# Layer norms with means in four PSUM banks and fewer filler matmuls, and the first shifted inputs of a local attention sent by the stage before it

## What is computed

```python
x = x + retention(layernorm(x))              # 16 heads, causal, no softmax
x = x + cross(layernorm(x), context)         # 16 heads, sigmoid scores
z = layernorm(x)
for l in range(2):
    h = shift_token(z)                       # upper half of the features moved one token on
    z = z + local_attention(h @ wqkv) @ wo   # windows of 64, 8 heads of 64, softmax
    h = layernorm(shift_token(z)) * lg + lb
    a, g = split(h @ w1 + b1)
    z = z + (a * gelu(g)) @ w2 + b2
x = x + z
```

## Time and profile before

| | |
|---|---|
| median of 3 runs | 1876.77 us (1872.91 to 1878.39) |
| profiled execution, its own time | 1873.96 us |
| its span | 1872.1 us |
| mean granted TensorE clock | 0.976 of 2.4 GHz |
| busy: TensorE, ScalarE, VectorE, GpSimd | 92%, 78%, 55%, 24% |

### The profile page before, as it was taken

One profiled execution on the slowest core, in us unless ns is written; L12 is line 12 of the kernel. 1 busy time (PEld: TensorE's weight loads), 2 busy tenths in 40 slices (PEclk: granted clock), 3 DMA queues, 4 the chain that ended last, 5 costly groups with the idle time before them and its releaser, 6 DMA issues. The chain is left out here.

```text
span 1872.1 us, 67917 instructions
## 1 busy us (share of the span) xinstructions
PE 1713.8 (92%) x28036; PEld 1024.3 (55%) x28036; DVE 1025.8 (55%) x3242; ACT 1462.7 (78%) x2635; POOL 445.5 (24%) x353
## 2 busy tenths in 40 slices
PE   7898799999998999999999968999989789889888
PEld 4675455555554555555555435666653256656633
DVE  4444633333332334333331069999964499899844
ACT  3332699999997999999999848999972389989832
POOL 1003100000000000000000047777710377767300
PEclk9998999999998999999999989999999999999999
DMA  1000211111111111111110021111110011111100
GB/s 59 3 3 26 104 48 50 60 43 61 62 62 35 57 54 49 56 62 62 52 39 17 27 82 27 35 31 25 28 27 0 11 27 24 35 29 26 32 15 34
DMA packets 47469, 73.88 MB, mean 39 GB/s; under 512 B 8400, under 2 KB 38224, under 8 KB 47184
## 3 DMA queue, kind: packets, MB, share of 16 engines
q1 hardware_dynamic: 47184, 69.85, 12.1%
HBM read 21.08 MB, written 2.10 MB: 12 GB/s over the span
## 5 line engine op out<-in xcount | busy, mean ns | idle before, releaser
L638 ACT ACTIVATE x_probs<-x_pss 128x1024 f32<-128x1024 f32 x832 | 806.3, 1021 | 51.7 <-PE x_pss L559 36.7
L573 PE MATMUL x_acc<-x_probs,x_v 128*32 128x256 f32 x6656 | 437.7, 380 | 0.1
L559 PE MATMUL x_pss<-x_qx,x_kx 32*128 32x256 bf16 x9984 | 348.4, 270 | 14.3 <-issue 6.5
L559 PEld LDWEIGHTS x_pss<-x_qx,x_kx 32*128 32x128 bf16 x9984 | 221.4, 93 | 200.0 <-ACT x_probs L638 179.8
L573 PEld LDWEIGHTS x_acc<-x_probs,x_v 128*32 128x32 f32 x6656 | 206.6, 110 | 93.3 <-issue 9.1
L1244 ACT ACTIVATE l_prob<-l_sim,l_neg_top,l_inv_norm 128x128 f32<-128x128 f32 x512 | 245.7, 487 | 5.7 <-DVE l_neg_top L1138 4.6
L685 DVE COPY x_vnext<-x_psp 128x128 f32<-128x128 f32 (+1 forms) x199 | 59.2, 298 | 315.3 <-PE x_psp L537 312.2
L870 POOL TENSOR_TENSOR l_turned_half<-l_raw,l_tabB 128x512 f32<-128x512 f32 x128 | 181.5, 1439 | 69.9 <-ACT l_raw L1203 69.6
L614 POOL COPY x_zq<-zT 128x256 f32 (+1 forms) x15 | 6.0, 400 | 763.7 <-PE x_psp L544 695.4
L880 POOL TENSOR_TENSOR l_direct<-l_direct,l_turned_half 128x1024 f32<-128x1024 f32 x64 | 156.1, 2439 | 0.0
L1130 DVE CUSTOM_DVE_ANT_0 l_sim<-l_pss,w_window 128x128 f32<-128x128 f32 x512 | 118.0, 285 | 4.3 <-issue 2.9
(11 more groups left out here) (177 smaller groups left out, 2636.6 us busy)
## 6 DMA issues: line engine op xcount, KB each, us to landing
x_kx<-x_kp SPq DMA_DIRECT2D x96, 208.0 KB, 2.3
x_cT<-in_context SPq DMA_DIRECT2D x16, 832.0 KB, 4.5
x_qx<-x_qp SPq DMA_DIRECT2D x48, 192.0 KB, 3.0
l_vmid<-l_vt SPq DMA_DIRECT2D x64, 128.0 KB, 2.3
xT<-in_x SPq DMA_DIRECT2D x8, 256.0 KB, 4.9
shifted<-zT SPq DMA_DIRECT2D x32, 64.0 KB, 2.0
hs<-zT SPq DMA_DIRECT2D x32, 64.0 KB, 2.0
out_x<-xT SPq DMA_DIRECT2D x8, 256.0 KB, 2.0
```

Of the source, the lines that this page charges most:

```text
L559: ins = pe.matmul(pss[bank(k, 2 * p + r // 2)][:, r % 2, e, :], kx[par][rows, g, j * P:(j + 1) * P], qx[par][rows, g, a * S:(a + 1) * S], ...
L573: ins = pe.matmul(acc[32 * r:32 * r + 32, 0:S], v[:, j, g, r, :], probs[SLOT[p]][r // 2][:, r % 2, e, :], start=(u == 0), stop=(u == UNITS ...
L638: act.activation(probs[SLOT[p]][y][:, :, :, :], pss[bank(k, 2 * p + y)][:, :, :, :], ACT.Sigmoid, scale=HD ** -0.5).then_inc(weighed, 1)
```

## The change

Means of norm 1 and norm 3 and of both gate stages go to four banks, the two of `mean` and the first two of `wide`; norm 2, which uses all of `wide` for its projection, keeps two. In all three norms the 8 filler matmuls ahead of `widen(0)` are gone. In the gate stages the wait for the second refinement moves behind `widen(0, 0)`. The copies for batches 0 to 3 of a local attention are issued by SyncE in the stage before: in norm 3 behind the weight loads and before the wait for them, in gate 0 as chunks 0 and 1 are added. The `landed` semaphores become four that both layers share.

```diff
+def shift_in(sp, shifted, zT, landed, n):
+    sp.dma_start(shifted[n % 4][0:64, :], zT[0:64, n * S:(n + 1) * S]).then_inc(landed[n % 4], 16)
+    sp.dma_start(shifted[n % 4][64:P, 1:S], zT[64:P, n * S:(n + 1) * S - 1]).then_inc(landed[n % 4], 16)
...
 # layer_norm
+        means = mean if project is not None else [*mean, wide[0], wide[1]]
+        MB = len(means)
...
                 for tile, dram in loads:
                     sp.dma_start(tile, dram).then_inc(landed, 16)
+                if next_shift is not None:
+                    shifted, batches_landed = next_shift
+                    sp.wait_ge(cleared, len(zeros))
+                    for n in range(4):
+                        sp.wait_ge(normed, base + n // 2 + 1)
+                        shift_in(sp, shifted, dst, batches_landed, n)
                 if loads:
                     sp.wait_ge(landed, 16 * len(loads))
...
-                if n >= 2:
-                    pe.wait_ge(centered, base + n - 1)
-                pe.matmul(mean[n % 2][:, :], ones_mean[:, :], src[:, at[n]], start=True, stop=True).then_inc(mean_ready, 1)
+                if n >= MB:
+                    pe.wait_ge(centered, base + n - MB + 1)
+                pe.matmul(means[n % MB][:, :], ones_mean[:, :], src[:, at[n]], start=True, stop=True).then_inc(mean_ready, 1)
...
             variances(1)
-            keep_warm(WARM)
             widen(0)
             keep_warm(WARM)
             widen(1)
...
 # local_attention
             def shift(n):
-                if n >= 4:
-                    sp.wait_ge(v_projected, 2 * n - 6)
...
+                sp.wait_ge(v_projected, 2 * n - 6)
+                shift_in(sp, hs, zT, landed, n)
...
-            for n in range(4):
-                shift(n)
             for n in range(B):
                 middle(n)
...
-                        pe.wait_ge(landed[r], 32 * (q + 1))
+                        pe.wait_ge(landed[r], 32 * (q + 1) + 32 * (B // 4) * layer)
...
 # norm_and_gate
+        means = [*mean, wide[0], wide[1]]
...
+        if next_shift is not None:
+            @block.sync
+            def _(sp):
+                for n in range(4):
+                    sp.wait_ge(added, runs + n // 2 + 1)
+                    shift_in(sp, next_shift[0], zT, next_shift[1], n)
...
-                if n >= 2:
-                    pe.wait_ge(centered, base + n - 1)
-                pe.matmul(mean[n % 2][:, :], ones_mean[:, :], hs[:, at[n]], start=True, stop=True).then_inc(mean_ready, 1)
+                if n >= 4:
+                    pe.wait_ge(centered, base + n - 3)
+                pe.matmul(means[n % 4][:, :], ones_mean[:, :], hs[:, at[n]], start=True, stop=True).then_inc(mean_ready, 1)
...
                     widen(0, 0)
+                    pe.wait_ge(newton, (run * NG + 1) * 2 + 2)
                     for c in range(4):
                         spread_out(1, c)
                     widen(0, 1)
...
-            pe.wait_ge(newton, (run * NG + 1) * 2 + 2)
             pe.wait_ge(centered, base + NCH)
             chunks(pe, chunk)
```

More of the change, by code:

```diff
@@ L36 @@
 NEG = -3.0e38
+def shift_in(sp, shifted, zT, landed, n):
+    sp.dma_start(shifted[n % 4][0:64, :], zT[0:64, n * S:(n + 1) * S]).then_inc(landed[n % 4], 16)
+    sp.dma_start(shifted[n % 4][64:P, 1:S], zT[64:P, n * S:(n + 1) * S - 1]).then_inc(landed[n % 4], 16)
 def layer_norm(nc, tag, norms, src, dst, loads=(), zeros=(), gain=None, source=None,
-               project=None, arrived=None):
+               project=None, arrived=None, next_shift=None):
     ones_mean, eps, pick, run = norms["ones_mean"], norms["eps"], norms["pick"], norms["runs"]
@@ L171, in _ @@
                 dve.wait_ge(mean_ready, base + n + 1)
-                dve.tensor_tensor(dst[:, at[n]], src[:, at[n]], mean[n % 2][:, :], ALU.subtract).then_inc(centered, 1)
+                dve.tensor_tensor(dst[:, at[n]], src[:, at[n]], means[n % MB][:, :], ALU.subtract).then_inc(centered, 1)
             refine(0)
@@ L740, in _, with local_attention @@
                 add(B - 1, c)
-def local_attention(nc, tag, zT, w, hs, moved_to, moved):
+def local_attention(nc, tag, zT, w, hs, moved_to, moved, landed, layer):
     KEYS = [[(0, P, 0, P)], [(WINDOW, WINDOW + P, 0, WINDOW), (P, S, WINDOW, P)]]
@@ L781, in local_attention @@
         pso = ps("pso", [P, PH, P])
-        ready, landed = sem("ready"), [sem(f"landed{r}") for r in range(4)]
+        ready = sem("ready")
         q_projected, k_projected, squared = sem("q_projected"), sem("k_projected"), sem("squared")
@@ L827, in shift @@
             def shift(n):
-                if n >= 4:
-                    sp.wait_ge(v_projected, 2 * n - 6)
-                sp.dma_start(hs[n % 4][0:64, :], zT[0:64, n * S:(n + 1) * S]).then_inc(landed[n % 4], 16)
-                sp.dma_start(hs[n % 4][64:P, 1:S], zT[64:P, n * S:(n + 1) * S - 1]).then_inc(landed[n % 4], 16)
+                sp.wait_ge(v_projected, 2 * n - 6)
+                shift_in(sp, hs, zT, landed, n)
             def middle(n):
@@ L1278, in _, with norm_and_gate @@
             turns(act, turn)
-def norm_and_gate(nc, tag, norms, gates, zT, hs, w, moved, layer, xT=None, out=None, stored=None):
+def norm_and_gate(nc, tag, norms, gates, zT, hs, w, moved, layer, xT=None, out=None, stored=None, next_shift=None):
     ones_mean, eps, pick, run = norms["ones_mean"], norms["eps"], norms["pick"], norms["runs"]
@@ L1441, in _ @@
                 dve.wait_ge(mean_ready, base + n + 1)
-                dve.tensor_tensor(hs[:, at[n]], hs[:, at[n]], mean[n % 2][:, :], ALU.subtract).then_inc(centered, 1)
+                dve.tensor_tensor(hs[:, at[n]], hs[:, at[n]], means[n % 4][:, :], ALU.subtract).then_inc(centered, 1)
             refine(0)
@@ L1496, in build @@
         stored = ctx.enter_context(nc.semaphore("stored"))
+        batches_landed = [ctx.enter_context(nc.semaphore(f"batch_landed{r}")) for r in range(4)]
         gates = [ctx.enter_context(nc.semaphore(f"gate_{n}")) for n in (
@@ L1546, in build @@
             layer_norm(nc, "n3", norms, xT, zT, loads,
-                       [x[:, :] for x in shifted])
+                       [x[:, :] for x in shifted], next_shift=(shifted, batches_landed))
             for l, w in enumerate(ws):
-                local_attention(nc, f"l{l}", zT, w, shifted, hs, moved)
+                local_attention(nc, f"l{l}", zT, w, shifted, hs, moved, batches_landed, l)
                 if l + 1 < DEPTH:
-                    norm_and_gate(nc, f"g{l}", norms, gates, zT, hs, w, moved, l)
+                    norm_and_gate(nc, f"g{l}", norms, gates, zT, hs, w, moved, l, next_shift=(shifted, batches_landed))
                 else:
```

## The result

The changed kernel took 1858.44 us (median of 5 runs, 1854.96 to 1863.45) against 1876.77: ratio 0.9893 with the 95% interval 0.9869 to 0.9916. The profiled execution took 1858.44 us, with a span of 1856.6 (before 1872.1) and a mean granted clock of 0.978.

What follows compares the result with a forecast made beforehand. Bound by short waits in the norms, gates and local attention starts, any gain there shifting what follows. Terms 2.2 + 1.96 + 2.3 + 2.4 + 2.5 + 0.65 = 12.0 us, from median 1876.77 to 1864.8; range 1859 to 1871.5.

Steps and rivals of the forecast that it cites:

- Norms, the filler: All three norms: the filler alone holds back group 0's spread; removing it gains 1.96 us in each.
- Norm 3 and its SyncE: Norm 3 into local attention 0: SyncE's copies end the stage, but the first matmul starts sooner; gain 2.3 us.
- the term of 2.5: Start of local attention 1: copies issued in gate 0 remove TensorE's 2.57 us wait for data; gain 2.5 us.
- if the shorter idle time spares this, 0.85 more: Start of local attention 1: 0.85 us extra if shorter idle time avoids the clock's fall near TensorE's restart.
- the term of 2.4: Gate 0: 0.3 us by order, 0.5 by banks and 1.65 by a spared low clock; taken as 2.4 us.
- The 0.3 for the order: Gates: running chunk 0's matmuls ahead of the wait for the second refinement wins at most 0.3 us.
- The 1.65 for the spared low clock: Gate 0: chunk 0's matmuls no longer run into the low clock after TensorE's idle time; 1.65 us.
- Gate 1: 0.65 forecast: Gate of layer 1: at most 0.3 us by order together with 0.4 by the banks, taken as 0.65 us.
- Norm 2: 1.96, which cross attention inherits as a shift: Norm 2 ends 1.96 us sooner without its filler, and cross attention merely starts that much earlier.
- The first: Rival: full queue in norm 3, low clock in gate 0, half of layer 1's start lost; 7.2 us gain, chance 0.20.
- The second: Rival: attention's pipeline absorbs the starts, SyncE eats norm 3; about 4.5 us gain, 1872.3, chance 0.10.
- The third: Rival: clock falls inside each norm without filler, 4.6 us in each, near 20 in all; 1884.8, chance 0.04.

Runs made afterwards that it cites:

- e1: Kernel before, with only the 8 filler matmuls ahead of the first spread removed in the three norms: 1872.27 us, ratio 0.9974.
- e6: The changed kernel measured once more, nothing altered: 1859.52 us, ratio 0.9907 to the kernel before.
- e8: Changed kernel, but norm 3 issues only batch 0's two copies and local attention 0 the other six at its start: 1857.5 us, ratio 0.9904.
- e11: e8 with `widen(0, 1)` put ahead of group 1's spread in the gates: 1853.54 us, ratio 0.9886.
- e2: Kernel before, with only the means in four banks (norms 1 and 3, both gates): 1871.69 us, ratio 0.9976.
- e5: The kernel before measured once more, nothing altered: 1879.14 us, ratio 1.0004.
- e3: Kernel before, with only the shift copies issued in the stage before: 1867.58 us, ratio 0.9944.
- e4: Kernel before, with only the gates' wait for the second refinement moved behind the first chunk's matmuls: 1876.14 us, ratio 0.998.
- e9: Kernel before, with the first 8 fillers of each norm made one column wide, same instruction count: 1881.35 us, ratio 1.0038.
- e10: Kernel before, with 8 one-column matmuls added behind each norm's second spread: 1878.36 us, ratio 1.0019.
- e7: Changed kernel, with 8 one-column matmuls added behind each norm's second spread: 1859.99 us, ratio 0.9928.
- e12: e11 with the norms' second 8 fillers dropped too: 1858.35 us, ratio 0.9902.

## Why the prediction was right and where it failed

**Norms, the filler: right.** From the start of the second variances to the end of norm 2 it is 10.79 us before and 8.81 after: 1.98 for the forecast 1.96. By whole stages, norm 2 measured 26.90 to 27.90 us without the first fillers (after, e1, e6, e8, e11), 28.85 to 29.82 with them (before, e2 to e5): means 27.6 and 29.4, a gain of 1.8, with the scatter of what stands ahead of the variances. Norm 1, with the banks, went from a mean of 29.11 (before, e3, e4, e5) to 26.43 (after, e6, e8, e11): 2.7 for 2.2, the surplus falling to the banks, where 0.4 to 0.7 was seen for 0.3.

**Norm 3 and its SyncE: the mechanism right, the size a little low.** From the start of norm 3 to the first matmul of local attention it was 20.97 + 2.62 = 23.59 us before and 20.63 + 0.04 = 20.67 after: 2.9 for 2.3. The 0.6 more is SyncE's weight loads, whose last issue ended 14.9 us into the stage, where it had been 15.5 (1087.19 - 1071.65). Over the 14 profiles it ended 13.7 to 16.2 us into the stage, so this part is chance. No run shows the full queue that the prediction names as a bound: no issue of a copy sent ahead took longer than 0.61 us. Norm 3 and local attention 0 together went from a mean of 320.2 (before, e5) to 317.0 (after, e6), 3.2.

**Local attention 1: the term of 2.5 was too small.** In seven kernels without the copies ahead, POOL's first product comes 5.83 to 7.17 us into the stage (mean 6.60); in seven with them 2.80 or 2.81. That is 3.8. I had most of the rest and put it aside: "if the shorter idle time spares this, 0.85 more". It spares it in all seven, and in four of the six others the start took longer than in the profile that I had. How much of it reaches the end of the stage is less sure: the means of the whole stage are 308.4 and 305.2 us, 3.2 less, and the kernels that ran it with 17.1 us at the low clock differ by 2.4 (before and e9 against e3, e6 and e8).

**Gate 0: the term of 2.4 was too large.** The gates with 3.4 us at the low clock, and none of it at chunk 0 except in the kernel before, took 84.92 to 85.12 without the change (before, e1, e3, e10) and 84.63 to 84.71 with it (after, e7, e8, e11, e12): 0.3, which is the banks. The 0.3 for the order is zero by e4 against e3. The 1.65 for the spared low clock was booked as certain. Its size was right (1.66 in e4), but before the edit the clock fell there in 5 of 14 gates only, so it is worth about 0.6 us a gate on average, in both layers (estimate: 1.65 times 5/14). The changed kernel has its low clock at the first means instead, which is chance too, and so the two profiles differ by only 0.45. The Trainium skill, page "TensorE: Matmul & The Clock Gate", section "Why this matters for your kernels", asks for no long idle gaps between bursts of matmuls. The traces agree as far as they go: behind 2.57 us the clock fell at chunk 0 in 5 gates of 14, behind 0.92 us in none of 14.

**Gate 1: 0.65 forecast,** 0.25 by the banks; the rest of the 1.84 between the two profiles goes with 3.6 us less at the low clock.

**"Norm 2: 1.96, which cross attention inherits as a shift": this is the step that failed.** The sum put the untouched stages at nothing, and cross attention is not shifted rigidly. In the kernels with the old split (8 or 9 records, then a second pause of 1.9 to 2.9 us: before, e2, e3, e4, e5, e7, e9) the batch behind the loop's return takes 59.97 to 62.11 us, mean 61.10; in those without it (after, e1, e6, e8, e10, e11, e12; a second pause of 0.40 to 0.98 in three, none over 0.2 in four) 56.82 to 59.41, mean 57.99. The gain of 3.1 had no term in my sum. Part of it is clock: the first group has 8.3 us low on average and the second 4.9. At the same 6.8 us low it is 60.4 (e2, e5, e7, e9) against 59.1 (after, e1, e8), 1.3 us. The other 1.8 goes with the clock; that the longer pause brings it about is likely, but no run separates the two. e7, e9 and e10 show that the number of TensorE instructions in front of the loop decides: with the old number the split is there though the fillers do other work; with eight fewer or eight more in each norm it is gone. The instruction blocks on q8 show the wait itself: in all ten kernels with a second pause, it ends 1.26 to 1.51 us behind the end of such a block, and the first pause ends 1.54 to 1.81 us behind one in all fourteen. The Trainium skill, page "Runtime: NRT & Kernel Launch", section "Instruction fetch mechanics", says that a taken branch to a page outside the loaded window stalls until that page is there, and that blocks are otherwise fetched ahead, mostly hidden. The first pause agrees. The second does not: the next block set out only 0.42 to 1.03 us after TensorE had resumed, and where the old one held just 8 or 9 more records its fetch was not hidden.

**The sum.** 2.7 + 1.8 + 3.2 + 3.1 + 3.8 + 0.3 + 0.25 makes 15.2 for the 12.0 forecast, with local attention 1 counted by its start. Measured are 17.1 (e6 against its own kernel before) to 20. (The four parts measured alone add up to 1.26%, the whole to 0.93 or 1.07%; the intervals of the parts, 0.2 to 0.3% each way, cover that.) What is left is 2 to 5 us. About 1.2 of it may be the falls at chunk 0 of the two gates (twice 0.6). The rest lies where stages differ in their time at the low clock, as in the first seven batches of cross attention (0.87 in the profiles); whether the change causes that, or chance, no run settles; nor did I follow up why two batches of local attention 1 take 16.3 us in some kernels and 18.5 to 19.9 in others (16.3 and 18.8 before, 19.8 and 16.3 after, so it nearly cancels here).

**The rivals.** The first (full queue, low clock staying in gate 0) came true in the two profiles in one of its three parts, gate 0. The second, starts hidden by the pipeline, falls: e3 alone gives 0.56%. The third, the clock falling within the norms, did not happen with the filler simply removed: in none of 21 norms does it fall between the second variances and the end of the first spread. e9 shows that its single prices were about right where the clock does fall (2.09 for 1.14 us, 3.78 for 2.05), but norm 3 lost 2.2 us by it and not 4.6. The range was too narrow below, because it held no term for the untouched stages.

## What to carry to other kernels

Before calling an untouched stage a rigid shift, look for loops whose return leaves a pause called "issue" in the profile, and for the "instruction" packets next to it: adding or removing instructions ahead of the loop in that engine's stream can bring a second pause or take it away. Do not book a spell of low clock seen in one execution as the certain cost of the code around it; look whether the same code runs at full clock in its sister stage or in a second execution, and book it by how often it falls there. When two kernels differ in a stage, cut the stage at the edit too: what stands ahead of the second variances scatters by 1.5 us and more in norm 3. When work moves into the stage before, add up the issues of the queue it lands on: here two copies ahead do as well as eight and leave the stage 2.0 us shorter.

## What I had not expected of the hardware

An f32 filler of one column costs nearly as much as one of 128 (1.95 against 2.05 us for 16 records at full clock), and behind it the clock fell in two norms of three (0.50 in the window above), where between the second variances and the end of the first spread it fell in none of the 18 norms with wide first fillers and in none of the 21 without first fillers. Shrinking the fillers was worse here than either keeping or removing them: e9 is 0.4% slower than the kernel before. And 32 records fewer ahead of cross attention, in a program of 28,000, took a pause of more than 2 us out of it. By the packets on q8, that pause is TensorE's wait for 16 KB of its own instructions.
